# A graph layer's third batch: scores in full against a crossed product turned through HBM

## The reference

```python
u = einsum('bld,bmd->blm', h, h) / sqrt(d)
p = softmax(u, axis=-1)
delta = p * adjacency
attn = delta / (sum(delta, axis=2, keepdims=True) + 1e-10)
ctx = attn_left @ h_left + diag_a * h_self + attn_right @ h_right   # above, on, below the diagonal
o = (ctx - mu) / sqrt(var + 1e-12) * gamma + beta
x = layernorm(x + relu(o))
```

## Time and profile before

| | |
|---|---|
| runs | 462.38 us median of 3 (462.02 to 462.85) |
| profiled execution | 462.62 us, span 460.9 us, 1.7 us around it |
| TensorE busy | 450.7 us, 98% |
| VectorE, ScalarE, GpSimd busy | 83%, 70%, 45% |
| TensorE clock | 0.995 of full over the span; 1.00 in every 5 us of the first 65 |
| HBM | 174 GB/s over the span |

### The profile page before, as it was taken

The page is one execution under the profiler, slowest core; times in us unless marked ns, Lnnn a source line. Parts: engine busy times, 40 slices in busy tenths (PEclk is TensorE's granted clock), DMA queues, the critical chain, the costliest instruction groups (busy, mean ns, idle before and its releaser), DMA issues.

```text
span 460.9 us, 9449 instructions
## 1 busy us (share of the span) xinstructions
PE 450.7 (98%) x2639; PEld 448.4 (97%) x2639; DVE 383.0 (83%) x1117; ACT 321.5 (70%) x710; POOL 209.4 (45%) x293
## 2 busy tenths in 40 slices
PE   8999999999999999999999999999999999999992
PEld 8999999999999999999999999999999999999992
DVE  5877888888888878988878988878889887987876
ACT  6756677677677677678677677677677777767752
POOL 0144445543345553345554345554344653344542
PEclk9999999999999999999999999999999999999998
DMA  8765356566455665555666555566445566454322
GB/s 255 225 206 181 118 178 195 189 196 192 144 180 184 189 193 173 174 171 182 188 193 198 152 172 183 183 206 193 154 159 194 176 216 193 144 175 141 102 70 79
DMA packets 84134, 80.59 MB, mean 175 GB/s; under 512 B 7058, under 2 KB 76436, under 8 KB 84116
## 3 DMA queue, kind: packets, MB, share of 16 engines
q1 hardware_dynamic: 84112, 80.38, 54.7%
q10 hardware_dynamic: 4, 0.00, 0.0%
HBM read 52.04 MB, written 28.31 MB: 174 GB/s over the span
## 4 chain that ended last, share of the span: by engine, by line
issue 28%; POOL 21%; DVE 14%; PE 14%; ACT 11%; DMA 6%; SPq 5%; POOLq 0%; DVEq 0%; ACTq 0%
PE ps_proj L484 8%; POOL scaled L1112 7%; POOL shifted L1116 6%; DMA dt_raw<-dt_dram 5%; POOL rstd L1106 5%; ACT normed L639 4%; SPq L321 3%; DVE y_sb L867 3%; ACT ps_scores L590 3%; DVE proj_lo L819 3%; PE ps_ctx L528 3%; POOL dt_right L1100 2%; DVE delta L799 2%; DVE cross_turned L767 2%; POOL dt_left L1100 2%
## 5 line engine op out<-in xcount | busy, mean ns | idle before, releaser
L484 PE MATMUL ps_proj<-w_hi,xt_split 128*128 128x384 f32 x1152 | 304.8, 336 | 0.1
L484 PEld LDWEIGHTS ps_proj<-w_hi,xt_split 128*128 128x128 f32 x1152 | 209.1, 188 | 0.7 <-ACT ps_proj L609 0.5
L484 PE MATMUL ps_proj<-w_lo,xt_split 128*128 128x384 f32 x576 | 193.6, 336 | 0.0
L1106 POOL TENSOR_TENSOR rstd<-var_eps,minus_half 128x4 f32<-128x4 f32 x31 | 36.5, 1177 | 187.8 <-DVE var_eps L853 187.8
L484 PEld LDWEIGHTS ps_proj<-w_lo,xt_split 128*128 128x128 f32 x576 | 108.3, 188 | 0.0
L609 ACT ACTIVATE ps_proj<-bias 128x386 f32<-128x386 f32 (+1 forms) x188 | 90.5, 495 | 1.5 <-DVE proj_lo L819 1.2
L1112 POOL TENSOR_TENSOR scaled<-normed,gamma_sb 128x384 f32<-128x384 f32 x60 | 61.0, 1017 | 30.2 <-ACT normed L639 30.2
L613 ACT ACTIVATE proj_hi<-ps_proj 128x384 fp32r<-128x384 f32 x128 | 63.5, 497 | 11.3 <-PE ps_proj L484 11.0
L633 ACT ACTIVATE ps_ctx<-ps_proj,diag 128x386 f32<-128x386 f32 x64 | 35.7, 557 | 49.1 <-PE ps_proj L484 49.1
L819 DVE TENSOR_TENSOR proj_lo<-ps_proj,proj_hi 128x384 fp32r<-128x384 f32 x128 | 67.4, 544 | 2.1 <-ACT proj_hi L613 2.1
L1116 POOL TENSOR_TENSOR shifted<-scaled,beta_sb 128x384 f32<-128x384 f32 x61 | 61.9, 1015 | 2.5
(11 more groups left out here) (104 smaller groups left out, 640.2 us busy)
## 6 DMA issues: line engine op xcount, KB each, us to landing
x_sb<-in_x SPq DMA_DIRECT2D x32, 384.0 KB, 4.3
xt_sb<-in_x_t SPq DMA_DIRECT2D x31, 384.0 KB, 3.9
out_dram<-out_sb SPq DMA_DIRECT2D x31, 384.0 KB, 2.8
adj_sb<-in_adj SPq DMA_DIRECT2D x32, 256.0 KB, 4.4
dt_dram<-turned SPq DMA_DIRECT2D x31, 256.0 KB, 2.0
dt_raw<-dt_dram SPq DMA_DIRECT2D x124, 64.0 KB, 2.0
cross_dram<-cross_turned SPq DMA_DIRECT2D x29, 256.0 KB, 2.0
cross_raw<-cross_dram SPq DMA_DIRECT2D x116, 64.0 KB, 2.0
```

What stands on the lines that cost most here:

```text
L484: mm = nc.tensor.matmul(ps_proj[bank(at, g)][:, 0:H], stationary, moving[w][:, c, :], start=(clear and i == 0), stop=True, skip_group_chec ...
L1106: nc.gpsimd.tensor_tensor(rstd[at.slot(2)][:], var_eps[:], minus_half[:], ALU.pow).then_inc(rstd_ready, 1)
```

## The change

`IN_FULL` goes from 3 to 2. Batch 2's scores, which were made in full in the middle of batch 1 (after its group 0), are made by `cross` between batch 0's two contexts; batch 3's `cross`, which stood after batch 1's group 4, goes between batch 1's two contexts. SP stores and loads the crossed tile of batch 2 around the turned one of batch 1. In batch 1, ScalarE and VectorE do the split of batch 3's input, and the exponentials, maxima and deltas of batch 2, later than before. From batch 2 on the order is as it was.

```diff
-    IN_FULL = 3
+    IN_FULL = 2
@@ sync, batch 0
                     store_turned(nxt)
+                    store_cross(ahead)
                     load_turned(nxt)
+                    load_cross(ahead)
@@ tensor, batch 0
                     attend(at, 0)
+                    cross(ahead)
                     attend(at, 1)
@@ tensor, other batches
                     project(at, g)
-                    if at.b == 1 and g == 0:
-                        scores_in_full(nxt)
                     if i == 3 and last(at):
                         attend(at, 0)
-                    if g == 4 and ahead.exists(BATCHES):
+                    if g == 4 and at.b != 1 and ahead.exists(BATCHES):
                         cross(ahead)
                 if not last(at):
                     attend(at, 0)
+                if at.b == 1:
+                    cross(ahead)
                 attend(at, 1)
@@ scalar, batch 1
                     normalise(before)
-                    split_xt(ahead)
-                    exps(nxt)
                     split_proj(at, 1)
                     seed_proj(at, 4)
                     split_delta(at)
+                    split_xt(ahead)
                     split_proj(at, 2)
                     seed_proj(at, 5)
+                    exps(nxt)
@@ vector, batch 0
                     context_stats(at, 0)
+                    turn_cross(ahead)
@@ vector, batch 1
                     split_proj(at, 0)
-                    finish_scores(nxt)
-                    split_xt(ahead)
-                    deltas(nxt)
                     split_proj(at, 1)
                     split_delta(at)
+                    split_xt(ahead)
                     split_proj(at, 2)
-                    turn(nxt)
+                    finish_scores(nxt)
+                    split_proj(at, 3)
                     residual(before, 0)
                     residual_stats(before, 0)
-                    split_proj(at, 3)
+                    deltas(nxt)
+                    turn(nxt)
                     turn_cross(ahead)
```

## The result

The changed kernel took 466.12 us, the median of six runs (465.37 to 467.65), against 462.2 us (461.72 to 463.03): a ratio of 1.0078, 95% interval 1.0057 to 1.0099. It was timed once more beside the experiments: 465.22 us, ratio 1.0057 (1.0044 to 1.0070). By the medians it is 3.9 us slower in the first set and 2.6 us in the second (462.59 us for the kernel before). Forecast were 464.3 us and a range up to 465.5; the direction was right, the size was not: the first median lies outside the range, the second just inside it.

A forecast was written before the change was run, and what follows sets the result against it. The prediction took TensorE's queue, matmuls busy 98% of the span, as the bound. Its terms, -0.89 + 1.50 + 0.34 + 0.72 + 0.25 = +1.92 us, gave 464.3 us, range 463.0 to 465.5.

The forecast's parts named there:

- what is saved: TensorE's queue: batch 2's full scores, 2.13 us, replaced by a crossed product of 1.24 us, 0.89 us shorter.
- the first batch: Between batch 0's contexts: deltas end at 22.10, TensorE reaches cross(2) at 22.86, so no wait.
- The hole before the first context: Before batch 1's first context: TensorE waits for its seed from 35.06 to 36.56, 1.50 us.
- the one before cross(3): Between batch 1's contexts: TensorE waits 0.34 us for batch 2's deltas, queued behind split (1,3), residual and statistics.
- The chain: ScalarE and VectorE steps from batch 0's normalise at 28.46 to seed_ctx(1,0), behind batch 2's exponentials, ending at 36.53.
- the collision: VectorE's split_delta(1) falls into GpSimd's addition of beta, 30.37 to 31.38, and loses 0.37 us under mutual exclusion.
- the other case: At split_delta(1): VectorE and GpSimd share at half speed, so the loss is about half of 0.37 us.
- a second collision: Rival, chance 0.13: GpSimd 0.3 us later makes VectorE's residual at 36.58 wait out an addition; +2.7 us, 465.1.
- the first term: Batch 2's turned loads issue 2.03 us after their store, at 41.23; TensorE waits 0.72 us before (2,4).
- the second term: The granted clock was taken as full; the sum had no term for the clock.
- the wait of 0.25 us before cross(4): In batch 2: batch 3's deltas come at 50.08, TensorE reaches cross(4) at 49.85, waiting 0.25 us.
- an upper bound of half a microsecond for late DMAs: Bound on the sum: the second stage's loads landing 0.5 us slower would give +2.6 us.

The follow-up runs named there:

- changed again: The changed kernel, no edit, timed once more beside the kernel before: 465.22 us, ratio 1.0057.
- crossed store behind: Changed kernel with SP in batch 1 issuing the crossed store after the loads of the turned tile, not before: 469.93 us, ratio 1.0146.
- hole filled: Changed kernel with twelve matmuls of zeros, 384 columns each, at the end of group (2,3), where TensorE otherwise waits: 466.77 us.
- small matmuls: Changed kernel with eight matmuls of zeros, 128 columns each, at the end of group (1,5): 465.65 us.
- longer hole: Changed kernel with four copies of 384 columns to a scratch tile on ScalarE ahead of seed (2,4): 468.57 us.
- warm-up: Changed kernel with four of the six warm-up matmuls, 384 columns wide, replaced by 24 of 128 columns: 470.65 us.
- seed first: Changed kernel with ScalarE's split (1,3) and seed_ctx(1,0) ahead of the exponentials of batch 2 in batch 1: 464.7 us.
- deltas first: Changed kernel with VectorE in batch 1 doing deltas and turn of batch 2 ahead of batch 0's first residual: 464.33 us.
- both orders: Changed kernel with seed_ctx(1,0) ahead of the exponentials and deltas and turn ahead of the residual in batch 1: 463.1 us, ratio 1.0012.
- third batch's order: As both orders, and in batch 2 ScalarE and VectorE split the turned deltas behind split (2,1), not first: 463.86 us.
- turn last: Changed kernel with VectorE's turn of batch 2 behind the turn of batch 3's crossed tile: 466.94 us.
- the kernel before with a wait of its own: Kernel before the change with eight copies of 384 columns to a scratch tile on ScalarE ahead of seed (2,4): 465.96 us.

## Why the prediction was wrong

**Right: what bounds, what is saved, and the first batch.** The 18 products went and nine came for them. From batch 1's first matmul to batch 2's it was 15.60 us (15.62 in the forecast), 15.91 before. cross(2) did not wait. The hole before the first context was 1.43 us by the starts (34.95 + 0.17 to 36.55), forecast 1.50; the one before cross(3) 0.23, forecast 0.34. The chain, the seed behind exponentials whose input comes late, is shown by the experiment that swaps the two: the hole goes and 1.45 us with it. The deltas behind the residual is shown by the other swap.

**Right in kind, with the loss on the other engine: the collision.** VectorE's split_delta(1) took 0.90 us instead of 0.69, from 31.09 on, beside the addition of beta; forecast was a loss of 0.37. GpSimd lost more, at its first triangle, 1.06 us against 0.41, beside the split of batch 3 (timelines of VectorE and of GpSimd, changed kernel):

```profile
31.09 0.90 DVE L832 TENSOR_TENSOR dt_full<-dt_raw,dt_full 128x512 fp32r<-128x512 f32 x1 [0.37 <-ACT dt_full L626]
31.92 0.94 DVE L762 TENSOR_TENSOR xt_split<-xt_sb,xt_split 128x768 fp32r<-128x768 f32 x1
```

```profile
30.43 1.01 POOL L1120 TENSOR_TENSOR shifted<-scaled,beta_sb 128x384 f32<-128x384 f32 x1
32.06 1.06 POOL L1104 TENSOR_SCALAR_AFFINE_SELECT dt_left<-dt_full 128x256 fp32r<-128x256 f32 x1 [0.62 <-DVE dt_full L832]
```

GpSimd's loss cost nothing, as the contexts wait longer for the seed; VectorE's 0.21 us stand in the chain to that seed. The Trainium skill, SBUF — State Buffer, Who interferes with whom, has the shared ports as an exclusive lock, where the order of issue decides who blocks. The second pair agrees: VectorE, which began first, took its usual 0.94 us, and GpSimd lost 0.65 of the 0.80 us for which the two overlapped. The first pair agrees only in who lost: 0.21 of 0.35 us, less than the whole that the forecast took and near the half that it named as the other case. The rival "a second collision" did not happen: GpSimd was through at 36.26, the residual began at 36.51.

**Wrong, the first term: "The loads of the turned deltas can be issued 2.03 us after the store, at 41.23".** It was 3.86 us in the profiled execution and 2.87 in the next. The place of the wait was right, before (2,4), but it was put at 0.72 us and measured 2.31 and 1.39. The distance of 2.03 us came from one row; nothing of the kernel before had a store of the turned tile beside an instruction packet, though a store of the crossed tile had one, and landed in 2.6 us. The runs show the cause:

| kernel | store issued | packet starts | behind the issue | landing |
|---|---|---|---|---|
| changed | 39.08 | 40.5 | 1.4 | 3.8 |
| changed again | 38.74 | 39.2 | 0.4 | 2.8 |
| crossed store behind | 41.42 | 41.9 | 0.5 | 3.3 |
| hole filled | 39.82 | 40.5 | 0.7 | 3.1 |
| small matmuls | 39.48 | 40.0 | 0.5 | 3.3 |
| longer hole | 41.28 | 41.8 | 0.5 | 2.9 |
| warm-up | 43.61 | 44.0 | 0.4 | 3.3 |
| seed first | 37.96 | 39.9 | 1.9 | 2.4 |
| deltas first | 38.57 | 40.3 | 1.8 | 2.1 |
| both orders | 37.62 | 39.3 | 1.7 | 2.0 |
| third batch's order | 37.88 | 39.6 | 1.7 | 2.0 |
| turn last | 40.49 | 38.8 | -1.7 | 2.0 |

Seven stores with the packet in their first 1.4 us land in 2.8 to 3.8 us, five without in 2.0 to 2.4. Moving the store ahead of the packet or behind it, by two different edits, both gave 2.0 to 2.1. The traces hold more stores than these: the fourteen profiles have 852 stores of this size, turned and crossed. In 16 of them a 16 KB packet starts within 1.5 us behind the issue, and all 16 land in 2.5 to 3.8 us; of the other 836, 813 land within 2.3 us. The other 23 took up to 3.2 us without such a packet, so it is not the only thing that can hold a store. How it does so is seen in the changed kernel's own trace: nine of the store's 144 packets, one engine's share, had not moved while the 16 KB were on an engine; in the profile with the deltas first 143 of the 144 had moved before the packet came. The trace doesn't number the engines, so that it was the same one is read from the counts; and both attempts to move the packet by itself failed. Nor is it fixed by the program: the same kernel had it 1.4 us behind the store in one execution and 0.4 in the next.

**Wrong, the second term: the sum had no clock in it.** "The granted clock is full" was taken over to a kernel with holes. Behind the 2.1 us wait the clock was granted at half for 3.41 us, which cost 1.66 us in that execution. That such a wait can do it is shown by the kernel before with a wait of its own. The filled hole can't tell: its six runs had a mean clock of 0.994 or more, but the changed kernel run beside it, with a shorter wait, had 0.993 or more too. What else decides is open: 2.42 us of wait passed without it in one profile, 2.14 and 2.20 did not, and near 11 us, while TensorE waited for weights, 0.91 and 1.00 us were enough in two profiles.

**Small: the wait of 0.25 us before cross(4).** There in the second profile (0.22 us), absent in the first, where (2,4) was slow enough to hide it. One thing more cost about 0.1 us at each wait and was in no term: the first matmuls behind a wait are 0.25 to 0.28 us apart, not 0.17. And the batches from 3 on ran without a new wait, as forecast. The kernel before lost 0.50 us in its last stage (the wait of the earlier trace rows is there, before a crossed product at 420.5), and the changed one didn't; this the sum didn't have.

Together for the profiled execution, against a span of 460.9: +1.30 to the end of batch 0 (1.24 of it cross(2)), -0.31 in batch 1, +3.98 in batch 2, -0.50 at the end, 4.47 of the 4.4 us by which the spans differ. In the second profile: +0.96, -0.30, +1.84, -0.50, 2.0 us. That this is nearly the forecast's 1.92 is luck: batch 2 lost 1.84 us where 0.97 were forecast, and 0.50 us at the end and 0.28 us ahead of the change (batch 0's last group starts at 19.44, against 19.72) made up for it. It was also the fastest of its five runs, 464.6 us; why the others, at nearly the same clock, took 465.05 to 465.58 us no trace shows. The range had an upper bound of half a microsecond for late DMAs and none for the clock.

## What to carry to other kernels

Where an engine is busy 98% of the time, work taken out of it is worth its length only if every chain that the removed work had covered is shorter than what is left; here 0.89 us of matmuls uncovered 1.7 us of waits in one batch and 1.6 us and more in the next. Work that an engine could do at once should not be queued behind work whose input is late: two swaps of neighbours took back 2.1 us of the loss and left the change 0.1% slower than the kernel before (1.0012), with no gain. Price a round trip through HBM by its worst rows, and give a wait of that size on TensorE the price of slower matmuls behind it.

## What the runs showed of the hardware

A store of 256 KB landed in 2.0 us as a rule and in 2.5 to 3.8 us in the 16 cases of fourteen profiles in which a 16 KB packet of the instruction queue started within 1.5 us behind its issue; one of them is in the kernel before, where the crossed store of batch 3, issued at 36.58 with such a packet at 36.7, took 2.6 us. Behind a wait of 2.1 to 2.7 us, TensorE's clock was at half, 1.2 of 2.4 GHz, for 3.41 us in three profiles and stayed full in a fourth, with 1.5 to 1.9 us between the runs of each kind in the changed kernel, the one with the turn last and the kernel before with the hole. One of 1.79 us, with another of 1.21 us 3.8 us later, came with 6.83 us at half; those of 1.1 to 1.6 us between 35 and 54 us were followed by none. Near 11 us a wait of 0.91 us and one of 1.00 us came with 3.41 us at half, so the length of the wait does not decide alone. Twenty-four matmuls of 128 columns at the start took 0.22 us each, eight of them at 35.5 us 0.12 us each, in place of the 0.06 us that I had taken for them at the start.
